# Inverse row sums spread through DRAM, and projections issued as two 64-column halves

## What is computed

```python
h = _layernorm(x, axis=-1) * (1 + ca) + sa
latent_kv = x @ w_kv_down                 # x is h here
kv = latent_kv @ w_kv_up
k, v = (kv[..., :HD], kv[..., HD:])
q = (x @ w_q).reshape(Bx, Tx, N_HEAD, HEAD_SIZE)
att = jnp.einsum('bqhd,bkhd->bhqk', q, k) * scale
att = jnp.where(causal, att, -jnp.inf)
att = jax.nn.softmax(att, axis=-1)
y = jnp.einsum('bhqk,bkhd->bqhd', att, v)
return y.reshape(Bx, Tx, HD) @ w_out
```

## Time and profile before

| | us |
|---|---|
| median of 3 runs | 1807.71 |
| lowest, highest run | 1806.67, 1811.2 |
| span of the profiled execution | 1806.0 |
| TensorE busy | 1747.4 |
| VectorE busy | 1256.8 |
| ScalarE busy | 890.7 |
| GpSimd busy | 854.1 |

### The profile page before, as it was taken

One profiled execution on the slowest core, in us unless ns is written; L12 is line 12 of the kernel. 1 busy time (PEld: TensorE's weight loads), 2 busy tenths in 40 slices (PEclk: granted clock), 3 DMA queues, 4 the chain that ended last, 5 costly groups with the idle time before them and its releaser, 6 DMA issues.

```text
span 1806.0 us, 40241 instructions
## 1 busy us (share of the span) xinstructions
PE 1747.4 (97%) x15846; PEld 1210.7 (67%) x15846; DVE 1256.8 (70%) x2775; ACT 890.7 (49%) x1970; POOL 854.1 (47%) x1282
## 2 busy tenths in 40 slices
PE   8999999999999999999999999999999999999998
PEld 5666675668566677566856667656685666766667
DVE  5888847626788885753678886675467888576445
ACT  5676624223577763322457675432246767443233
POOL 2777842221187873241138787314114877631420
PEclk9999999999999999999999999999999999999999
DMA  6555570321255554040135555305014555520500
GB/s 185 130 134 125 126 220 14 53 42 38 72 134 133 126 120 143 1 81 14 37 95 132 127 130 132 111 2 94 1 43 109 134 128 122 132 98 2 94 1 26
DMA packets 120188, 164.48 MB, mean 91 GB/s; under 512 B 30305, under 2 KB 87105, under 8 KB 118977
## 3 DMA queue, kind: packets, MB, share of 16 engines
q1 hardware_dynamic: 106032, 155.09, 35.8%
q10 hardware_dynamic: 13968, 6.82, 1.3%
HBM read 63.22 MB, written 4.24 MB: 37 GB/s over the span
## 4 chain that ended last, share of the span: by engine, by line
PE 77%; DVE 10%; ACT 5%; SPq 3%; DMA 2%; issue 1%; POOL 1%; ACTq 0%; DVEq 0%; POOLq 0%
PE bank L680 11%; PE scores L462 11%; PE scores L660 10%; PE bank L462 7%; PE bank L715 4%; SPq L998 3%; DVE prob L809 3%; PE scores L1763 2%; ACT prob L920 2%; PE scores L1673 2%; PE bank L721 2%; PE bank L717 2%; PE scores L1116 2%; PE scores L1735 2%; PE scores L1185 2%; PE scores L433 2%
## 5 line engine op out<-in xcount | busy, mean ns | idle before, releaser
L878 POOL COPY placed<-prob 32x768 f32<-32x768 f32 x384 | 315.5, 822 | 27.5
L291 POOL TENSOR_TENSOR rstd<-rstd,minus_half 128x2 f32<-128x2 f32 x96 | 69.7, 728 | 542.0 <-DVE rstd L290 539.9
L680 PEld LDWEIGHTS bank<-placed,v_t 128*64 128x64 f32 x4608 | 251.6, 137 | 73.9 <-issue 68.3
L680 PE MATMUL bank<-placed,v_t 128*64 128x128 f32 x4608 | 274.4, 276 | 8.1 <-DMA placed<-hx 4.7
L660 PE MATMUL scores<-k_t,q_t 64*128 64x512 f32 (+3 forms) x1536 | 275.1, 496 | 0.8 <-ACT rec_t L930 0.8
L802 DVE CUSTOM_DVE_ANT_0 mod_rows<-scores,hx 128x128 f32<-128x128 f32 (+7 forms) x256 | 191.7, 749 | 75.7 <-PE scores L660 75.7
L809 DVE STREAM_TRANSPOSE prob<-prob 128x1536 f32<-128x1536 f32 x128 | 222.9, 1765 | 27.4 <-ACT prob L920 27.2
L802 DVE CUSTOM_DVE_ANT_0 x<-scores,hx 128x128 f32<-128x128 f32 (+7 forms) x256 | 192.7, 753 | 0.0
L920 ACT ACTIVATE prob<-mod_rows,neg_max 128x128 f32<-128x128 f32 (+2 forms) x192 | 137.4, 716 | 102.9 <-DVE neg_max L802 81.9
L660 PEld LDWEIGHTS scores<-k_t,q_t 64*128 64x128 f32 x1536 | 129.5, 186 | 85.1 <-issue 62.0
L866 POOL COPY rec_wide<-rec 128x128 f32<-128x128 f32 x256 | 64.9, 289 | 226.0 <-DVE rec L813 167.9
(11 more groups left out here) (262 smaller groups left out, 3392.1 us busy)
## 6 DMA issues: line engine op xcount, KB each, us to landing
placed<-prob SPq DMA_DIRECT2D x640, 96.0 KB, 2.2
f<-in_L_ffn_f SPq DMA_DIRECT2D x16, 2048.0 KB, 13.6
placed<-hx SPq DMA_DIRECT2D x320, 96.0 KB, 2.2
mod_rows<-mod_scratch SPq DMA_DIRECT2D x32, 128.0 KB, 4.5
out<-x SPq DMA_DIRECT2D x16, 256.0 KB, 2.1
w_ring<-in_L_attn_w_q ACTq DMA_DIRECT2D x24, 128.0 KB, 2.5
w_ring<-in_L_attn_w_kv_up ACTq DMA_DIRECT2D x48, 64.0 KB, 2.0
next_x<-in_L_attn_x SPq DMA_DIRECT2D x6, 512.0 KB, 4.6
```

Source lines behind the costliest of these rows:

```text
L291: step = pool.do(lambda e, ts=ts: nc.gpsimd.tensor_tensor(rstd[:, ts], rstd[:, ts], minus_half[:, ts], op=ALU.pow), var, filled)
L680: last = nc.tensor.matmul(out_bank[rows_, at_:at_ + P], v_t[pair % 2][:, j, rows_], placed[m % 2][:, :, head, first_block(m, i) + j, :], s ...
L878: nc.gpsimd.tensor_copy(placed[m % 2][target * GROUP:(target + 1) * GROUP, source, :, :, :], prob[m % 3][source * GROUP:(source + 1) * GRO ...
```

## The change

It has two parts.

**Inverse row sums.** The sums of a whole pair are kept (`row_sum` is 128 x 2 x 16). Once a pair, in the round with m % 3 = 2, VectorE takes one reciprocal between the two `shuffle` instructions and, behind the second, one 32 x 32 block transpose of 128 x 32. ScalarE stores the result to a scratch in DRAM at the end of the round (`store_inverse`). In the next pair's first round, behind six exponentials, it reads it back with two DMAs, one per head, each a row of 1024 values to 64 partitions (`spread_inverse`, into `inverse_wide`, of which there is one). `widen`, `turn_inverse` and `copy_rec` are gone. `norm` runs four rounds late, ahead of `keep(m)`. The output products begun early take six pairs rather than seven.

**Projections.** Each product of a job is issued as two with 64 columns of weights each, which write the two halves of PSUM's partitions, as the values' products do.

```diff
@@ pe_pairs
-            def turn_inverse(m):
-                e.wait_ge(flow["widened"], base["widened"] + m + 1)
-                e.wait_ge(flow["masked"], base["masked"] + parts_through(min(m + 1, ROUNDS - 1)))
-                if m > 0:
-                    e.wait_ge(flow["rec_copied"], base["rec_copied"] + m)
-                for k in range(len(tiles_in(m))):
-                    last = nc.tensor.transpose(rec_bank[:, k * P:(k + 1) * P], rec_wide[:, k, :], ident[:, :])
-                last.then_inc(flow["rec_turned"], 1)
...
                 if kind == "q":
                     for c in range(C):
-                        last = nc.tensor.matmul(ps, ring[:, c * P:(c + 1) * P], hT[:, c, cols], start=c == 0, stop=c == C - 1)
+                        for side in ROWS_OF:
+                            last = nc.tensor.matmul(ps[side, :], ring[:, c * P + side.start:c * P + side.stop], hT[:, c, cols],
+                                                    start=c == 0, stop=c == C - 1)
                 elif kind == "k":
-                    last = nc.tensor.matmul(ps, ring[:, 2 * P:3 * P], latT[:, cols], start=True, stop=True)
+                    for side in ROWS_OF:
+                        last = nc.tensor.matmul(ps[side, :], ring[:, 2 * P + side.start:2 * P + side.stop], latT[:, cols],
+                                                start=True, stop=True)
...
-                e.wait_ge(flow["normed"], base["normed"] + OUT_ROUND[tile] - ROUNDS_OF + 1)
+                e.wait_ge(flow["normed"], base["normed"] + ROUNDS_OF * BEGUN)
...
-                for j in range(PAIRS - 1):
+                for j in range(BEGUN):
...
-                if m > 0:
-                    turn_inverse(m - 1)
@@ dve_pairs
+            def invert(pair):
+                e.wait_ge(flow["exp_done"], base["exp_done"] + PARTS_OF * (pair + 1))
+                nc.vector.reciprocal(inverse[:, 0:HEADS * T], row_sum[:, pair % 2, :]).then_inc(flow["inverted"], 1)
+
+            def turn_inverse(pair):
+                e.wait_ge(flow["inverted"], base["inverted"] + pair + 1)
+                if base["inverse_stored"] + pair:
+                    e.wait_ge(flow["inverse_stored"], base["inverse_stored"] + 16 * pair)
+                nc.vector.transpose(inverse_t, inverse).then_inc(flow["inverse_turned"], 1)
...
-                for head in range(HEADS):
-                    shuffle(m, head)
-                invert(m)
+                shuffle(m, 0)
+                if m % ROUNDS_OF == ROUNDS_OF - 1:
+                    invert(m // ROUNDS_OF)
+                shuffle(m, 1)
+                if m % ROUNDS_OF == ROUNDS_OF - 1:
+                    turn_inverse(m // ROUNDS_OF)
@@ pool_pairs
             def norm(m):
-                e.wait_ge(flow["kept"], base["kept"] + len(COPIES) * min(m + 2, ROUNDS))
-                e.wait_ge(flow["rec_copied"], base["rec_copied"] + m + 1)
+                pair = m // ROUNDS_OF
+                e.wait_ge(flow["kept"], base["kept"] + len(COPIES) * min(m + NORM_LAG, ROUNDS))
+                e.wait_ge(flow["inverse_spread"], base["inverse_spread"] + 16 * HEADS * (pair + 1))
                 e.wait_ge(flow["values_read"], base["values_read"] + m + 1)
...
             for m in range(ROUNDS):
                 if m > 0:
                     e.wait_ge(flow["kept"], base["kept"] + len(COPIES) * m)
-                widen(m)
+                if m >= NORM_LAG:
+                    norm(m - NORM_LAG)
                 keep(m)
-                if m > 0:
-                    norm(m - 1)
-            norm(ROUNDS - 1)
+            for m in range(ROUNDS - NORM_LAG, ROUNDS):
+                norm(m)
@@ act_pairs
+            def store_inverse(pair):
+                e.wait_ge(flow["inverse_turned"], base["inverse_turned"] + pair + 1)
+                e.dma_start(inverse_dram[pair % 2].rearrange("k (a i) -> a k i", a=GROUPS), inverse_t
+                            ).then_inc(flow["inverse_stored"], 16)
+
+            def spread_inverse(pair):
+                e.wait_ge(flow["inverse_stored"], base["inverse_stored"] + 16 * (pair + 1))
+                if pair > 0:
+                    e.wait_ge(flow["normed"], base["normed"] + ROUNDS_OF * pair)
+                for head, rows_ in enumerate(ROWS_OF):
+                    e.dma_start(inverse_wide[rows_, :], inverse_dram[pair % 2, head * T:(head + 1) * T, :].rearrange(
+                        "k i -> (k i)").partition_broadcast(HD0)).then_inc(flow["inverse_spread"], 16)
...
+                if m > 0 and m % ROUNDS_OF == 0:
+                    spread_inverse(m // ROUNDS_OF - 1)
                 if m in (1, 3):
                     job(*jobs[0])
                 exponential(m, large, 0)
...
-                if m > 0:
-                    copy_rec(m - 1)
+                if m % ROUNDS_OF == ROUNDS_OF - 1:
+                    store_inverse(m // ROUNDS_OF)
             read_values(ROUNDS - 2)
-            copy_rec(ROUNDS - 1)
+            spread_inverse(PAIRS - 1)
             read_values(ROUNDS - 1)
```

More of the change, by code:

```diff
@@ L488, in batch @@
         placed = [part(f"placed{k}", [P, GROUPS, HEADS, BLOCKS, GROUP]) for k in range(2)]
-        rec_t = [part("rec_t", [P, 4 * P]), tmp[:, 0:2, :].rearrange("p t n -> p (t n)")]
-        rec_wide = part("rec_wide", [P, 4, P])
+        inverse_wide = part("inverse_wide", [P, S])
+        inverse, inverse_t = tmp[:, 0, 0:32], tmp[:, 0, 32:64]
         wq_dram = I["L0_attn_w_q"].rearrange("(c p) n -> p c n", p=P)
@@ L589, in out_parts, with out_place @@
             return [(0, 2)] if len(tiles_in(m)) == 2 else [(0, 3), (3, 4)]
-        def out_place(m, lo, hi):
+        def out_place(m, lo, hi, row=None):
             tiles = sorted(tiles_in(m))
             step = tiles[lo + 1] - tiles[lo] if hi - lo > 1 else 1
-            return by_tile(yT[:, m // ROUNDS_OF, :])[:, tiles[lo]:tiles[hi - 1] + 1:step, :]
+            return by_tile(yT[:, m // ROUNDS_OF, :] if row is None else row)[:, tiles[lo]:tiles[hi - 1] + 1:step, :]
+        NORM_LAG = 4
+        BEGUN = PAIRS - 2
         def by_tile(ap):
@@ L887, in norm @@
                     dst = out_place(m, lo, hi)
-                    last = nc.gpsimd.tensor_tensor(dst, dst, by_tile(rec_t[m % 2][:, lo * P:hi * P]), op=ALU.mult)
+                    last = nc.gpsimd.tensor_tensor(dst, dst, out_place(m, lo, hi, inverse_wide), op=ALU.mult)
                 last.then_inc(flow["normed"], 1)
@@ L913, in exponential @@
             def exponential(m, i, head):
-                k = column_of(m, i, head)
+                k, pair, sum_at = column_of(m, i, head), m // ROUNDS_OF, head * T + tiles_in(m)[i]
+                if m % ROUNDS_OF == 0 and i == 0 and head == 0 and pair > 1:
+                    e.wait_ge(flow["inverted"], base["inverted"] + pair - 1)
                 if i == 0 and head == 0 and b * ROUNDS + m > 2:
@@ L1099, in batch, with last_products, emit @@
         SPARE_TMP = 2
-        def last_product(ps, t):
-            return lambda e: nc.tensor.matmul(ps, yT[:, PAIRS - 1, t * P:(t + 1) * P], wout[:, PAIRS - 1, :], start=False, stop=True,
-                                              skip_group_check=True)
+        def last_products(ps, t, first):
+            def emit(e):
+                for j in range(first, PAIRS):
+                    last = nc.tensor.matmul(ps, yT[:, j, t * P:(t + 1) * P], wout[:, j, :], start=False, stop=j == PAIRS - 1,
+                                            skip_group_check=True)
+                return last
+            return emit
         def y_ready(t, pair=PAIRS - 1):
```

55 lines of the change are left out of this document (18 added, 37 removed).

## The result

The changed kernel takes **1885.56 us** (median of 4 runs, 1882.98 to 1887.44) against 1807.19 us for the kernel before on the same chip: ratio 1.0426 (95% interval 1.0411 to 1.0441). Forecast were 1837 us and a range of 1812 to 1862. Slower is right and the stop on ScalarE is there, but the loss is more than twice the forecast one: the profiled span is 1881.7 us, 75.7 us longer, where the sum had 29.

What follows compares the result with a forecast made beforehand. TensorE, busy 97%, was taken as the bound, with VectorE 2.46 us a pair behind. Five pairs a batch at +1.35 us (6.8) plus 0.5 at its end, times 4 batches, made +29 us: 1837 us, range 1812 to 1862.

Steps and rivals of the forecast that it cites:

- the stop on ScalarE: In a pair's first round the spread waits for GpSimd's norm of the pair before, delaying the seventh exponential by 3.65 us.
- the issues: ScalarE's two spread DMA issues, ahead of the seventh exponential, priced at 0.7 us from weight loads of 0.335 us each.
- VectorE's own loop: VectorE's time for a pair: 25.07 us, less 2.46 of waits for TensorE, plus 3.65 of ScalarE's delay, 26.26 us.
- The step that failed: Following ScalarE's delay to its waiters, through VectorE and the moves: 26.4 us for both paths, +1.35 us a pair.
- What remains of TensorE's gain is idle time on TensorE: TensorE's own need falls by 1.5 us to 23.6 us a pair; the rest of the longer pair it idles.
- The end of a batch: Later output products, the last spread's wait and the last turns' removal together: +0.5 us a batch, from -0.5 to +2.
- The two first pairs: In each batch's first two pairs the spread's issues, 0.7 us, eat what TensorE gives: 0.
- Rival (a): The spread's wait on ScalarE is short, a pair is TensorE's 23.6 to 23.8 us: 1782 us, chance 0.11.
- Rival (c): On TensorE the projections' column halves do not overlap or load their weights bare: +160 us, 1970 us, chance 0.03.
- Rival (d): The spreads' 512 KB a pair hold up the ten moves every round, so values wait: 1860 to 1890 us, chance 0.04.
- The halves: Queries' and keys' projections on TensorE in two column halves: no difference, from -0.2 to 0.5 us a pair.
- What would show it: Signs: pair 26 to 27 us, ScalarE idle over 2.5 us, VectorE's late transpose, TensorE idle 2 to 3 us a pair.

Runs made afterwards that it cites:

- the late spread: The changed kernel with the spread issued on ScalarE behind the reads of round A's jobs, not ahead of the seventh exponential: 1802.19 us, ratio 0.998.
- two other kernels: The changed kernel with store and query weights behind the first two exponentials, 1889.65 us; the changed kernel with whole-array projections, second try, 1906.46 us.

## Why the prediction was wrong in size, point by point

- **The stop on ScalarE** was right in place, cause and order. Forecast at t0 + 7.0, measured t0 + 7.40. The term off is the issues: 0.67 us for two, taken from a weight load, measured 0.47 and 0.61 us (with their gap 1.12). The copies and the product end at t0 + 6.15 (forecast 6.2), and the 0.1 for the semaphore, for which the sum names no row, is 0.08 (583.01 to 583.09). With this stop VectorE's own loop, 26.26 in the sum, is the 26.7 of the kernel that reads the values first.
- **The step that failed** stands behind the list "Queued behind it: that exponential, the reading of values, the eighth exponential, the reading of both query halves". Of their waiters it names two: "VectorE waits at the first transpose", "and TensorE for VectorE's least values in the next rounds". The sum followed the stop through VectorE, and through the moves, but not through the bank that the reading of values sets free. Who waits for that copy: the queries' second half, half a job ahead of its scores. Rows at hand gave it: t0 + 7.0 for the stop's end, then the exponential's 0.92 and the copy; and TensorE's queue from there. With the forecast stop, 0.4 us earlier, this loop is 26.9 us and not the sum's 26.4; against 25.07, times 20, that makes 37 us and not 27. The size of the issues makes it 45 (43.4 against the measured mean of 25.17).
- **"What remains of TensorE's gain is idle time on TensorE"** was priced at nothing. It is one idle time of some 3 us in each pair, and behind eleven of these twenty TensorE runs at half clock for a while: 19 us in the late pairs, and more at the ends. No term of the sum stood for it.
- **The end of a batch**, +0.5 us, is +3.4 from the last t0 to the next batch's first. TensorE there, in the changed kernel, idles 3.76 us for a move and runs the values at half clock:

```profile
234.49 4.17 PE L684 MATMUL bank<-placed,v_t 128*64 128x128 f32 x48 [3.76 <-DMA placed<-hx]
```

- **The two first pairs**: forecast 0, measured +1.2 a batch.
- **Rival (a)**, 1782 us if the wait were short, was priced too low for the stop alone: with the stop gone and the moves unhindered it is 1795.7. The 1784.2 near its figure needed a second edit that the rival doesn't have (store and weights behind the first exponentials), so the near hit is luck; late pairs there take 23.8 to 24.9 us (forecast 23.6 to 23.8). **Rival (c)** is out. **Rival (d)** is true in kind where nothing covers the moves, with the late spread's 5.51 us, but not as a cause in the changed kernel: its moves are waited for 24 us in all, less than its wait for `yT`.
- **The halves** at no difference: right in the kernel before. With the turns gone and TensorE nearly full they are worth 8.8 us; 0.47 us a pair is near the 0.63 that the sum took for three changes of form.
- **What would show it**: the late transposes are there (t0 + 8.46), the ScalarE idle time too (2.79 us). TensorE's 2 to 3 us were looked for before values and scores, and stood before the queries' second half: that place named the error at once. Released by the norm is right, though the row says "issue", since ScalarE's own DMA issues end it.

## What to carry to other kernels

When an in-order queue gets a stop, list every instruction behind it with its waiter, copies that only free a buffer included, and close each such loop separately; the longest need not pass through the engine one is looking at. Put a DMA that waits for another engine where that engine is surely done, behind the transfers that are urgent, and put issues without haste behind an engine's first useful work: the same change went from 4.3% slower to 1.25% faster by the position of its DMAs and of one weight load. And price idle time on TensorE by what its clock does afterwards, as a range: the same wait cost nothing in one pair and 1.3 to 2.9 us in the next.

## What the runs showed of the hardware

- A DMA issue on ScalarE's queue is not one price: 0.335 us for a 64 KB load, 0.65 for the query weights, 0.57 for the 16 KB store, 0.47 and 0.61 for the two spreads of the pair shown.
- A 256 KB spread over 64 rows lands in a median of 4.0 us; two of them beside the last of ten moves kept the 16 DMA engines busy nearly throughout, and the last move landed 3.1 us later than without them (4.85 us against 1.72 from its issue to the values).
- Idle times of 2.6 to 3.6 us in front of the same job of TensorE cost its clock in eleven of twenty pairs of the changed kernel and left it whole in nine: 3.38 us left it whole (667.73), 2.64 us did not (1596.39). In two other kernels, with waits of 2.2 to 3.7 us in the same place, it was sixteen and seventeen of twenty.
- Halves of 64 columns load their weights under running products: 16 products of 512 columns in halves took 3.63 us where 8 on the whole array took 3.70 (574.58, 575.73), and the kernel before took the same time with either (ratio 1.0004).
